# Attention and FFN block on one core: the seam between turns in another order, and the reciprocals of the row sums on VectorE

## The reference

```python
h = layernorm(x) * (1 + ca) + sa
qkv = einsum('bsh,ph->bsp', h, weight_qkv)            # 4 groups of 4 q, 1 k, 1 v, 128 wide each
scores = einsum('bgqsd,bgtd->bgqst', q, k) * 128 ** -0.5   # causal mask
x = x + ga * (softmax(scores) @ v) @ weight_proj.T
h = layernorm(x) * (1 + cb) + sb
x = x + gb * ffn(h)                                   # 256 -> 2 x 1024 -> 256, fwht before and after
```

## Time and profile before

| | us |
|---|---|
| median of 3 runs (1033.22 to 1034.03) | 1033.82 |
| the profiled execution | 1033.74 |
| its span, from the first to the last instruction | 1032.0 |
| mean granted clock of TensorE, share of full speed | 0.972 |

### The profile page before, as it was taken

One profiled execution on the slowest core, in us unless ns is written; L12 is line 12 of the kernel. 1 busy time (PEld: TensorE's weight loads), 2 busy tenths in 40 slices (PEclk: granted clock), 3 DMA queues, 4 the chain that ended last, 5 costly groups with the idle time before them and its releaser, 6 DMA issues.

```text
span 1032.0 us, 14510 instructions
## 1 busy us (share of the span) xinstructions
PE 965.7 (94%) x5344; PEld 831.5 (81%) x5344; DVE 659.1 (64%) x1290; ACT 521.4 (51%) x1085; POOL 459.5 (45%) x601
## 2 busy tenths in 40 slices
PE   6689998999799979998999899989998999999997
PEld 5569886988698869886888689868986898788885
DVE  6667756774677557745775577556755676874443
ACT  2266545664566356644764466456645665431221
POOL 4366605770577047804780378127722855220000
PEclk9889998999999989998999999999999999999999
DMA  8000100000000000000000000000000002000000
GB/s 298 21 1 1 31 1 21 2 31 1 21 1 32 1 19 4 31 1 1 21 31 1 0 22 31 1 1 22 1 1 0 2 1 82 1 1 21 20 20 20
DMA packets 9522, 21.14 MB, mean 20 GB/s; under 512 B 1264, under 2 KB 5488, under 8 KB 9328
## 3 DMA queue, kind: packets, MB, share of 16 engines
q1 hardware_dynamic: 8592, 19.66, 5.8%
q10 hardware_dynamic: 864, 0.60, 0.2%
HBM read 18.17 MB, written 2.10 MB: 20 GB/s over the span
## 4 chain that ended last, share of the span: by engine, by line
PE 83%; DVE 9%; ACT 5%; issue 2%; DMA 1%; SPq 0%; DVEq 0%; POOL 0%; ACTq 0%
PE ps L858 18%; PE ps L860 17%; PE ps L859 17%; PE ps L972 12%; PE ps L952 7%; PE ps L958 6%; PE ps L955 6%; DVE ps L760 3%; ACT prob L554 2%; DVE xhat L679 1%; ACT h L519 1%; DVE v_lo L740 1%; DMA x<-in_x 1%; ACT h_hi L519 1%; DVE q_lo L734 1%
## 5 line engine op out<-in xcount | busy, mean ns | idle before, releaser
L760 DVE CUSTOM_DVE_ANT_0 ps<-ps,mask_f 128x1024 f32<-128x1024 f32 (+7 forms) x256 | 195.2, 762 | 88.6 <-PE ps L958 85.6
L764 DVE TENSOR_TENSOR pt_lo<-ps,pt_hi 128x512 fp32r<-128x512 f32 x288 | 198.4, 689 | 73.7 <-ACT pt_hi L572 71.4
L554 ACT ACTIVATE prob<-ps,nmax 128x1024 f32<-128x1024 f32 (+7 forms) x256 | 189.8, 742 | 99.3 <-DVE nmax L760 98.6
L435 POOL TENSOR_TENSOR rinv<-rsum,mone 128x1 f32<-128x1 f32 x256 | 140.8, 550 | 213.9 <-ACT prob L554 212.5
L572 ACT ACTIVATE pt_hi<-ps 128x512 fp32r<-128x512 f32 x288 | 172.0, 597 | 112.9 <-PE ps L972 112.1
L438 POOL TENSOR_SCALAR prob<-prob,rinv 128x1024 f32<-128x1024 f32 (+7 forms) x256 | 192.3, 751 | 53.3 <-POOL rinv L435 53.3
L972 PE MATMUL ps<-ident,prob 128*128 128x128 f32 x1152 | 172.4, 272 | 0.0
L972 PEld LDWEIGHTS ps<-ident,prob 128*128 128x128 f32 x1152 | 142.0, 140 | 21.1
L952 PE MATMUL ps<-k_hi,q_hi 128*128 128x512 f32 (+4 forms) x384 | 125.4, 382 | 32.4 <-ACT prob L554 31.8
L858 PE MATMUL ps<-pt_hi,v_hi 128*128 128x512 f32 x288 | 135.2, 469 | 1.3 <-DVE pt_lo L764 1.3
L860 PE MATMUL ps<-pt_hi,v_lo 128*128 128x512 f32 x320 | 126.3, 395 | 0.0
(11 more groups left out here) (134 smaller groups left out, 1702.4 us busy)
## 6 DMA issues: line engine op xcount, KB each, us to landing
w_raw<-in_wqkv SPq DMA_DIRECT2D x8, 768.0 KB, 4.3
wp_raw<-in_wproj SPq DMA_DIRECT2D x8, 512.0 KB, 3.5
x<-in_x SPq DMA_DIRECT2D x4, 512.0 KB, 10.0
prob<-in_wug SPq DMA_DIRECT2D x4, 512.0 KB, 4.5
out_y<-prob SPq DMA_DIRECT2D x4, 512.0 KB, 2.9
prob<-in_wmod SPq DMA_DIRECT2D x1, 1024.0 KB, 10.0
raw_down<-in_wdn SPq DMA_DIRECT2D x1, 1024.0 KB, 14.2
prob<-in_wmod SPq DMA_DIRECT2D x1, 512.0 KB, 5.4
```

The lines of the kernel that those rows point to most:

```text
L554: a_.activation(row(i, h).rearrange("p (a n) -> p a n", a=nb), score_banks(i, h).rearrange("p (a n) -> p a n", a=nb)[:, :, 0:w], ACT.Exp, ...
L760: v_.tensor_tensor_reduce(scores, scores, late, -1.0, 3.0e38, ALU.add, ALU.min, nmax[:, place(n), h:h + 1]).then_inc(max_done, 1)
L764: v_.tensor_tensor(pt_lo[:, n % 3, :], T[n % 2], pt_hi[:, n % 3, :].bitcast(F32), ALU.subtract).then_inc(ptl_done, 1)
```

## The change

1. **The walk.** The four scores of row 7 of the next turn move into the last window, one beside each of its last four units, with `LN` behind the second. The 12 chunks stand in the first five units of the window (3, 3, 2, 2, 2) in place of all nine. After the last unit the order is now: `Y` of row 3, row 0 head 0, `VT`, row 0 head 1, `Y` of row 4, `WP`, `L`, row 0 heads 2 and 3, `LL`, two scores of row 6, first unit. ACT does a held-back exp also ahead of `VT` and `L`.
2. **Turn 0.** The scores of row 7 stand between chunks 6 to 9, and chunks 4 to 11 go to the two `X` banks, each waiting for the chunk two before it; chunks 4 and 5 wait only for DVE's constants.
3. **The reciprocal.** DVE takes it in place of POOL, with its own instruction, in a list `summed` that it empties after each chunk, each row maximum (of the scores before) and each unit's low part. It waits there for the exp (`exp_done`). POOL keeps the scaling.

```diff
@@ -53,6 +53,9 @@
     return min(i, NT - 1 - i)
+CHUNKS_AT = (3, 3, 2, 2, 2)
+
+
 def walk():
@@ -62,16 +65,21 @@
-    out = [(0, "LF", 0, 0)] + [(0, "C", c, 0) for c in range(NC)]
+    out = [(0, "LF", 0, 0)]
     def scores(t, i):
         return [(t, "S", i, h) for h in range(QPG)]
+    out += [(0, "C", c, 0) for c in range(6)]
+    for h in range(QPG):
+        out += [(0, "S", NT - 1, h), (0, "C", 6 + h, 0)]
+    out += [(0, "C", 10, 0), (0, "LN", 0, 0), (0, "C", 11, 0)]
     for t in range(TURNS):
-        last = [(t - 1, "Y", WINDOWS[-1][0], 0)] if t else []
-        s7, s0, s6 = scores(t, NT - 1), scores(t, 0), scores(t, NT - 2)
-        out += s7[:1] + last + [s7[1], (t, "VT", 0, 0), s7[2], (t, "LN", 0, 0), s7[3], (t, "L", 0, 0)]
-        out += [(t, "WP", 0, 0)] * (t > 0) + s0 + [(t, "LL", 0, 0)] + s6[:1]
+        s0, s6 = scores(t, 0), scores(t, NT - 2)
+        out += [s0[0], (t, "VT", 0, 0), s0[1]]
+        if t:
+            out += [(t - 1, "Y", WINDOWS[-1][0], 0), (t, "WP", 0, 0)]
+        out += [(t, "L", 0, 0), s0[2], s0[3], (t, "LL", 0, 0), s6[0]]
         behind, due = [], []
         def value():
@@ -91,9 +99,14 @@
                 for k, item in enumerate([item for i in WINDOWS[p + 1] for item in scores(t, i)][p == 0:]):
                     fill[k].append(item)
             elif t + 1 < TURNS:
-                for c in range(NC):
-                    fill[c * len(units) // NC].append((t + 1, "C", c, 0))
-                fill[4].append((t + 1, "LF", 0, 0))
+                chunks = [(t + 1, "C", c, 0) for c in range(NC)]
+                for k, many in enumerate(CHUNKS_AT):
+                    fill[k] += chunks[:many]
+                    del chunks[:many]
+                for h, item in enumerate(scores(t + 1, NT - 1)):
+                    fill[len(CHUNKS_AT) + h].append(item)
+                fill[1].append((t + 1, "LF", 0, 0))
+                fill[6].append((t + 1, "LN", 0, 0))
             if p in (1, 2) and t + 1 < TURNS:
                 fill[3].append((t, "W", 0, 0) if p == 1 else (t + 1, "WM", 0, 0))
             for n, extra in zip(units, fill):
...
@@ -269,7 +281,9 @@
             return (t + 1) * per[s.name] + k
-        def bank(c):
+        def bank(t, c):
+            if t == 0 and c >= 4:
+                return X[c % 2]
             return S[c % 4 // 2][:, c % 2 * CH:(c % 2 + 1) * CH]
         def nth(c):
...
@@ -431,8 +444,6 @@
                 e = scored(i, h)
                 at = place(i)
-                pool.wait_ge(exp_done, this(exp_done, t, e))
-                g_.tensor_tensor(rinv[:, at, h:h + 1], rsum[:, at, h:h + 1], mone[:, :], ALU.pow).then_inc(rinv_done, 1)
                 pool.wait_ge(rinv_done, this(rinv_done, t, e))
                 pool.sem_inc(pool_gate, 1)
                 g_.tensor_scalar(row(i, h), row(i, h), rinv[:, at, h:h + 1], 1.0, ALU.mult, ALU.mult).then_inc(prob_done, 1)
...
@@ -561,8 +572,10 @@
                     chunk(t, n)
                     exps()
                 if what == "VT":
+                    exps()
                     v_high(t)
                 if what == "L":
+                    exps()
                     ln_modulate(1, t // NKV, t % NKV, 0)
                 if what == "S":
                     exps()
...
@@ -741,9 +754,19 @@
                                      v_hi[:, 4 * n:4 * n + 4, :].rearrange("p j d -> p (j d)").bitcast(F32),
                                      ALU.subtract).then_inc(v_lo_s, 1)
+            summed = []
+
+            def reciprocals():
+
+                while summed:
+                    t, i, h = summed.pop(0)
+                    dve.wait_ge(exp_done, this(exp_done, t, scored(i, h)))
+                    v_.reciprocal(rinv[:, place(i), h:h + 1], rsum[:, place(i), h:h + 1]).then_inc(rinv_done, 1)
+
             for t, what, n, h in WALK:
                 if what == "C" and CHUNKS[n][0] != "v":
                     chunk(t, n)
+                    reciprocals()
                 if what == "VT":
                     v_low(t)
                 if what == "LF":
@@ -759,10 +782,13 @@
                     late = mask_f[:, SEQ - nb * w:SEQ].rearrange("p (a n) -> p a n", a=nb)
                     v_.tensor_tensor_reduce(scores, scores, late, -1.0, 3.0e38, ALU.add, ALU.min,
                                             nmax[:, place(n), h:h + 1]).then_inc(max_done, 1)
+                    reciprocals()
+                    summed.append((t, n, h))
                 if what == "T":
                     dve.wait_ge(pth_done, this(pth_done, t, n + 1))
                     v_.tensor_tensor(pt_lo[:, n % 3, :], T[n % 2], pt_hi[:, n % 3, :].bitcast(F32),
                                      ALU.subtract).then_inc(ptl_done, 1)
+                    reciprocals()
                 if what == "V" and n == LAST[UNITS[n][0]]:
                     i = UNITS[n][0]
                     dve.wait_ge(oh_done, this(oh_done, t, FINISHED.index(i) + 1))
@@ -911,12 +937,16 @@
                     pe.wait_ge(exp_done, this(exp_done, t, 0))
                     pe.wait_ge(w_ready, t + 1)
                     pe.wait_ge(ln[1]["lo"], t + 1)
-                if c >= 4:
+                if t == 0 and c == 4:
+                    pe.wait_ge(consts, 1)
+                elif t == 0 and c >= 6:
+                    pe.wait_ge(*evicted(t, c - 2))
+                elif t and c >= 4:
                     pe.wait_ge(*evicted(t, c - 4))
                 at = {"q": h, "k": QPG, "v": QPG + 1}[what] * D
                 start = t // NKV * SEQ + half * CH
                 for k in range(KH):
-                    last = three(bank(c), w_hi[:, k, at:at + D], w_lo[:, k, at:at + D],
+                    last = three(bank(t, c), w_hi[:, k, at:at + D], w_lo[:, k, at:at + D],
                                  h_hi[:, k, start:start + CH], h_lo[:, k, start:start + CH], k == 0, k == KH - 1)
                 last.then_inc(qkv_done, 1)
@@ -939,10 +969,14 @@
                 if what == "S":
                     e = scored(n, h)
-                    if e <= 2:
+                    if e <= 2 and t:
                         for c in (NC - 4, NC - 3) if e == 1 else (NC - 2, NC - 1):
                             pe.wait_ge(*evicted(t, c))
-                    else:
+                    elif e <= QPG and not t:
+                        pe.wait_ge(*evicted(t, e + 1))
+                    elif e == 5 and not t:
+                        pe.wait_ge(*evicted(t, NC - 1))
+                    if e > 2:
                         pe.wait_ge(exp_done, this(exp_done, t, e - 2 if n >= CT or h < 2 else e - 4))
                     nb, w = halves(n)
                     wide = max(w, 2 * P)
@@ -977,7 +1011,7 @@
                     if j == 0 and t == p == 0:
-                        pe.wait_ge(consts, 1)
+                        pe.wait_ge(*evicted(t, NC - 2 if i >= CT else NC - 1))
                     elif j == 0 and i >= CT:
                         pe.wait_ge(add_done, this(add_done, t, 2 * p - 1))
                     elif j == 0:
```

More of the change, by code:

```diff
@@ L175, in build @@
         mhalf = sb("mhalf", [P, LP])
-        mone = sb("mone", [P, 1])
         su_u = sb("su_u", [P, KH])
@@ L262, in build @@
         PER_ACT = {qkv_hi: 10, vt_done: 2, v_hi_s: 2, exp_done: 32, pth_done: NU, oh_done: NT}
-        PER_DVE = {qkv_lo: 10, v_lo_s: 2, max_done: 32, ptl_done: NU, ol_done: NT, add_done: NT}
-        PER_POOL = {prob_done: 32, rinv_done: 32}
+        PER_DVE = {qkv_lo: 10, v_lo_s: 2, max_done: 32, rinv_done: 32, ptl_done: NU, ol_done: NT, add_done: NT}
+        PER_POOL = {prob_done: 32}
         per = {s.name: n for d in (PER_PE, PER_ACT, PER_DVE, PER_POOL) for s, n in d.items()}
@@ L373, in _ @@
             pool.sem_inc(wp_ready, 1)
-            g_.memset(mone[:, :], -1.0)
             g_.memset(mhalf[:, :], -0.5).then_inc(pool_self, 1)
@@ L538, in chunk @@
                 if what == "v":
-                    a_.activation(vt[:, span], bank(c), ACT.Copy).then_inc(vt_done, 1)
+                    a_.activation(vt[:, span], bank(t, c), ACT.Copy).then_inc(vt_done, 1)
                 elif what == "k":
-                    a_.activation(k_hi[:, span], bank(c), ACT.Copy).then_inc(qkv_hi, 1)
+                    a_.activation(k_hi[:, span], bank(t, c), ACT.Copy).then_inc(qkv_hi, 1)
                 else:
-                    a_.activation(q_hi[:, h, span], bank(c), ACT.Copy, scale=SCALE).then_inc(qkv_hi, 1)
+                    a_.activation(q_hi[:, h, span], bank(t, c), ACT.Copy, scale=SCALE).then_inc(qkv_hi, 1)
             waiting = []
@@ L731, in chunk @@
                 if what == "k":
-                    v_.tensor_tensor(k_lo[:, span], bank(c), k_hi[:, span].bitcast(F32), ALU.subtract).then_inc(qkv_lo, 1)
+                    v_.tensor_tensor(k_lo[:, span], bank(t, c), k_hi[:, span].bitcast(F32), ALU.subtract).then_inc(qkv_lo, 1)
                 else:
-                    v_.scalar_tensor_tensor(q_lo[:, h, span], bank(c), SCALE, q_hi[:, h, span].bitcast(F32),
```

(1 more changed line is left out.)

## The result

The changed kernel takes 1037.74 us (median of six runs, 1035.23 to 1037.85), the kernel before 1033.61 us beside it (six runs, 1033.22 to 1034.71): a ratio of 1.0034, with a 95% interval of 1.0021 to 1.0047. It is slightly slower. The profiled execution took 1037.79 us with a span of 1036.0 us, 4.0 us more than the span of before.

What follows compares the result with a forecast made beforehand. PE was taken to bound the kernel, full in the windows with holes only in the seam. 1033.74 + 7.0 for seven seams - 2.4 for turn 0 gave 1038.3 us; range 1023 to 1053, the forecast's own 1036 to 1046.

Steps and rivals of the forecast that it cites:

- the loop: DVE waits for ACT's exp before each reciprocal, so long scores take 2.71 us each against PE's 2.52 us unit.
- the two new waits: In each seam PE waits 1.7 us before the last `V` and 1.2 us before `Y` of row 3.
- `LN` held back: `LN`'s second instruction may be held by POOL's scaling, stretching 0.79 to 1.9 us; 0.6 us a seam taken.
- Second and third windows at nothing: The loop costs nothing in a turn's second and third windows, since PE looks at an exp only two scores later.
- The first holes: PE waits at the end of the last window: 1.7 us on `pt_lo`, 1.2 us on `o_lo`.
- Row 6 and the first window: PE waits 2.5 us before row 6's first scores, then 1.0 and 1.1 us in the first window.
- The clock: PE's clock falls at the seam's holes, costing 2.2 us a seam, bounds 0 and 5.
- One seam: Each seam: -1.8 for waits, +0.6 for `LN`, +2.2 for the clock: +1.0 us, bounds -1.8 and +4.3.
- Turn 0: Start-up turn: row 7's scores start at 39.9, row 6's at 64.2 against 66.61; -2.4 us, bounds -4 and -0.5.
- the reciprocal held by GpSimd's operations: Rival, chance 0.06: POOL's long operations hold DVE's reciprocal, PE 2 to 3 us later in all eight turns; 1058 us.
- That the clock holds: Rival, chance 0.27: TensorE keeps 2.4 GHz in most seams or falls once, `LN` not held; 1019 to 1028 us.
- Its seam at -1.8 us before the clock: Seam waits at full clock sum to 7.5 us against 9.3 lost before, 1.8 us less, without held `LN`.

Runs made afterwards that it cites:

- filled kernel: The changed kernel with 6, 4 and 8 unread 128x512 matmuls in the three holes of each seam: 1019.40 us, 0.9860 of the kernel before.
- the later reciprocal: The changed kernel with VectorE taking each score's reciprocal one item later, same engine and instruction: 1004.46 us, 0.9714 of the kernel before.
- the walk alone: The changed kernel's new walk with the reciprocals left on GpSimd: 1005.84 us, 0.9733 of the kernel before.
- the old order: The walk of the kernel before, with the reciprocals moved to VectorE as in the change: 1041.63 us, 1.0071 of the kernel before.

## Why the prediction was right

1038.3 us was forecast and 1037.74 measured, by the mechanism that was forecast: the loop, the two new waits and a falling clock. That the number fits to 0.6 us is partly luck. In a seam the forecast had 8.1 us of waits (`LN` held back among them) and 2.2 of clock; the first seam shows 5.1 us of waits and up to 3.4 of clock, and the rest is in no term. The waits were thus put 3.0 us a seam too large, some 21 us over seven, against a forecast of +7.0 for all seven; the clock and that rest made it good.

- *The loop.* Forecast 2.71 us for a 1024-wide score, measured 2.62 to 2.64. That VectorE idles there before each reciprocal shows in 0.73 us each time, and moving the wait removed it. Shown.
- *Second and third windows at nothing.* Right: 20.00 of 20 us in each (192 to 212 and 212 to 232 us).
- *The first holes.* The wait on `pt_lo` was forecast at 1.7 us plus 0.6 for a held `LN`, and is 1.66. `LN` itself took 1.55 to 1.57 us in all seven seams (forecast 1.4, between 0.8 and 1.9), so the 0.6 was about right and the 1.7 beside it too large by 0.6 to 0.8; loops 0.07 us shorter explain 0.2 of that, the rest I can't place. The wait on `o_lo` was forecast at 1.2 and is 0.94.
- *Row 6 and the first window.* Forecast 2.5 and 2.1, measured 1.86 and 0.62. The second is the worst-sized wait. Part of it was hidden: the loop of 2.47 us was set against PE's work at full speed, while PE ran part of that stretch at 1.2 GHz and so had less to wait for. The filled kernel, with the same early reciprocal at the full clock, shows what that hid, 1.20 us in two waits where the forecast had 1.0 and 1.1. So of the 1.5 us too much, 0.6 is the clock and 0.9 the reading itself, which took the whole of the loop's excess as a wait; and the first of the two waits stands at 0.71 us with the later reciprocal too, so it isn't the loop's alone.

```profile
171.72 0.67 PE L991 MATMUL ps<-k_hi,q_hi 128*128 128x448 f32 x2 [0.72 <-ACT prob L566]
177.98 0.38 PE L991 MATMUL ps<-k_hi,q_hi 128*128 128x256 f32 x1 [0.48 <-ACT prob L566]
```

- *The clock.* Forecast 2.2 us a seam. The two stretches at 0.83 are 3.4 us each at the lower level, which costs up to 3.4 us of work together (20 x 0.17), and filling the holes gave back 2.6 a seam. The cost is real and was put too low by 0.4 or more; before, 16 us at 0.79 could cost as much (up to 3.4). In this seam the clock thus took about what it took before, while the forecast held that part of the fall would go.
- *One seam.* Waits 5.1 and clock 3.4 after, waits 4.6 and clock 3.4 before; with the clock at the most that it can cost, 1.6 and 1.3 us are left over that my sum of PE's work doesn't hold. The difference by the turns' clock is +0.8 us, forecast +1.0.
- *Turn 0.* Row 7's first scores start at 39.86 (forecast 39.9) and row 6's at 64.29 (forecast 64.2); by the first residual addition the turn gained 1.7 us instead of 2.4.

Of the rivals, the reciprocal held by GpSimd's operations did not come: 256 of them last 152 to 166 ns, and 66 of these start while a GpSimd instruction runs. One beside `wp_lo`, from the timelines of GpSimd and VectorE:

```profile
170.03 2.38 POOL L441 TENSOR_TENSOR wp_lo<-wp_raw,wp_hi 128x1024 fp32r<-128x1024 f32 x1
170.13 0.17 DVE L764 RECIPROCAL rinv<-rsum 128x1 f32<-128x1 f32 x1 [1.44 <-ACT prob L565]
```

That the clock holds was a rival with a chance of 0.27, and the filled kernel shows what it would have been: 1019.4 us, at the edge of its 1019 to 1028.

What the prediction did not see is the size of what was covered up. Its seam at -1.8 us before the clock was all that the order seemed to be worth, when the walk alone is worth 28 us (by the residual additions of its profiled execution, 81.7 to 846.2 us, 3.9 a seam and 2.8 in turn 0) and the early reciprocal takes more than that back. It had both parts in one sum, and never priced the walk without the loop.

## What to carry to other kernels

When a small operation moves to another in-order engine, price its place in that queue before the instruction: an instruction of 0.16 us was free here, its wait for an engine that had itself just waited for this one cost 31 to 33 us (7.6 in the old order), more than half of it through TensorE's clock, and taking it one item later cost nothing. Price each half of a two-part change by itself, for a sum near zero can be a good part and a bad one. At a wait, read what stands ahead of the awaited instruction on the engine that is waited for: two exponentials of 0.37 us put before four evictions (0.56 us each, 0.45 from one start to the next) were worth 17 to 19 us.

## What the runs showed of the hardware that was not expected

- VectorE's `RECIPROCAL` of 128x1 takes 152 to 166 ns in all 256 cases, the 66 that start beside a GpSimd instruction too, where the normalising `TENSOR_SCALAR` took 395 to 1239 ns. The Trainium skill ("SBUF — State Buffer", "Who interferes with whom") names the kinds that are held, and not the reciprocal; the trace agrees. In all seven seams the second of the two `TENSOR_SCALAR` meets GpSimd's scaling of 1.13 us, and the pair takes 1.55 to 1.57 us.
- The same hole lowers the clock in one seam and not in the next. With the later reciprocal TensorE waits 1.88 us before row 6's first scores in the first seam (they start at 166.01) and in the fourth (470.67), and is busy for 2.1 us of the 4 around that wait in both. Then the granted clock stays at 1.00 in the first and is 0.59 in the fourth; it fell behind this wait in five of the seven seams. What decides between them I did not find. First the stretches of the first seam, then those of the fourth:

```profile
162.00:166.00 4.00, 2.13 (x19) 1.92 (x17) 2.35 (x12) 2.87 (x10) 1.97 (x5) 1.00 0.01 2
166.00:170.00 4.00, 3.28 (x17) 2.79 (x18) 2.54 (x7) 1.57 (x5) 3.69 (x4) 1.00 0.21 33
```

```profile
467.00:471.00 4.00, 2.12 (x18) 1.90 (x17) 2.16 (x12) 2.98 (x10) 2.24 (x4) 1.00 0.01 2
471.00:475.00 4.00, 4.00 (x15) 3.50 (x14) 1.51 (x4) 1.10 (x2) 3.45 (x4) 0.59 0.25 58
```
